# Narrower expert slots in a fused attention and mixture-of-experts layer: 32 places of 256 columns for 16 of 512

## The chip, the core and the metric

The kernel runs on one core of a Trainium2 chip. The core has a matrix engine (TensorE, PE in the profile, with its weight loads as PEld), a vector engine (DVE), a scalar engine (ACT), GpSimd (POOL) and SyncE (SP), which here only starts transfers. The metric is the device time of one execution in microseconds. Every number format on the matrix engine here is 32 bit; each product is made of three passes over a high and a low part of the operands.

## The reference

The input is 8 sequences of 512 tokens with 512 features. Attention and its two layer norms come first; nothing of that part is touched. The second half, for 4096 tokens, 8 experts and two picks a token, is:

```python
logits = x @ router_weight.T
probs = softmax(logits);  top_v, top_i = top_k(probs, 2);  top_v = top_v / top_v.sum(-1)
for e in range(8):                       # I_MOE = 352
    gu = x @ gate_up_proj[e].T
    gate, up = gu[:, :352], gu[:, 352:]
    out += (silu(gate) * up @ down_proj[e].T) * combine[:, e:e+1]
out += sigmoid(x @ shared_gate_w.T) * (silu(x @ sh_gate_w.T) * (x @ sh_up_w.T) @ sh_down_w)   # 1408 wide
```

## The kernel before

Four stages follow one another, each in a block of its own with a barrier between: attention, routing (`build_routing`), experts (`build_experts`), the shared expert (`build_shared`).

**Slots and places.** Each of the 8192 picks gets a slot, so that the slots of one expert are contiguous within a tile. How many picks an expert has is known only at run time; the widths of the tiles are fixed in the program. Routing cuts the picks of an expert into whole tiles of TS = 512 and a rest, gives the whole tiles the first places (16 of them, `FULL`), and the rests, largest first, the last seven, whose widths 448, 384, ... 64 are what the j-th largest rest can at most be. `NT` is the number of places (23), `BLOCKS` the number of 128-slot blocks of each, `SC` their sum (80). Routing computes in one chain of small VectorE steps the expert of each place (elements NT x 8) and the slot of each pick, and then the inverse, token of slot, with 64 matmuls of SC columns (L1112). GpSimd first fills constants, among them one by one `place_base` and `tile_place` (L1078, L1080), NT memsets each.

**The expert stage.** `PLACE_OF` is the order in which places are worked on: 8 full ones in a loop of pairs (`LOOPED`), then written out, rests and full ones in turn. A tile n of w slots goes as follows.

- GpSimd gathers the rows of xn of its tokens, one indirect transfer for each block of 128 (L1466), into `xg`, two tiles ahead.
- TensorE transposes them (L1274), 4 transposes a block, in groups T0 to T3 for the four chunks of 128 features. ScalarE copies each chunk out as the high part (L1280, `high_x`), VectorE subtracts to get the low part (L1285, `low_x`). There is one `xT`, so this can only be written after the last gate and up product of the tile before has read it.
- Gate and up for three chunks c of the 352 hidden rows: 2 x 12 matmuls of w columns for each c (L1251). ScalarE takes silu (L1294), VectorE multiplies and splits (L1301, L1308, L1310).
- Down: 3 matmuls of 512 columns for each block and c (L1263), into `out_ps`; ScalarE copies each block to `y_out` (L1547), and SyncE stores it to `ys`.
- Meanwhile the weights of tile n + 1 are split into high and low parts, in seven pieces on ScalarE (L1357) and VectorE (L1361); the weights of tile n + 2 are loaded by SyncE, three transfers of together 2.1 MB, issued behind the store of tile n - 1 (L1343 to L1346).

The order of TensorE in a turn is written out by hand: gate and up 0, gate and up 1, down 0, gate and up 2, T0 and T1 of the next tile, down 1, T2 and T3, down 2. T2 and T3 wait for the split of hidden chunk 2 (their banks). The first gate and up product of tile n + 1 waits for all four `low_x` of tile n + 1. VectorE's order at the end of a turn is: multiply and split hidden chunk 2, two weight pieces, four `low_x`; ScalarE's: silu of chunk 2, two weight pieces, four `high_x`, the copies of the output.

**The seam to the shared stage.** In the last turn SyncE issues the first loads of the shared stage: x of sequences 0 and 1 (4 transfers of 1 MB, `load_x`, L1385) and the first two weight chunks (6 transfers of 256 KB, `load_weights`, L1391 to L1393), and behind them the store of the last tile.

Of the kernel before, what the change touches and what calls it, by code (L numbers as in the profile page):

```python
# [26 lines left out]
P = 128  # L27
S = 512
# [34 lines left out]
def blocks_before(n):  # L63

    return BLOCKS_BEFORE[n] if isinstance(n, int) else QT * n


def width(n):
    return WIDTH[n] if isinstance(n, int) else TS


def blocks(n):
    return BLOCKS[n] if isinstance(n, int) else QT

# [930 lines left out]
def build_routing(nc, logits, gate, weight, slot, token_of_slot, tile_expert, weights):  # L1005
# [6 lines left out]
    with ctx:  # L1012
# [105 lines left out]
        def _(dve):  # L1118
# [44 lines left out]
            steps.then_wait(nc.vector.tensor_copy(whole_i[:, 2, :], n_of))  # L1163
            nc.vector.tensor_scalar(whole_i[:, 0, :], whole_i[:, 2, :], TS.bit_length() - 1, None, ALU.logical_shift_right)
            steps.then_wait(nc.vector.tensor_scalar(whole_i[:, 1, :], whole_i[:, 2, :], TS - 1, None, ALU.bitwise_and))
            nc.vector.tensor_copy(ends[0][:], whole_i[:, 0, :])
# [30 lines left out]
            steps.then_wait(nc.vector.tensor_reduce(shift_rest[:], at_place[:], AX_X, ALU.add))  # L1197
            steps.then_wait(nc.vector.tensor_scalar(whole[:, 0, :], whole[:, 0, :], float(TS), None, ALU.mult))
            steps.then_wait(nc.vector.tensor_tensor(shift_rest[:], shift_rest[:], whole[:, 0, :], ALU.subtract))
            steps.then_wait(nc.vector.tensor_scalar(shift_whole[:], first[:], float(TS), None, ALU.mult))  # L1200
            steps.then_wait(nc.vector.tensor_tensor(shift_rest[:], shift_rest[:], shift_whole[:], ALU.subtract))
# [194 lines left out]
def build_experts(nc, xn, weights, ys, token_of_slot, stored, stage, idf):  # L1396

    ctx = ExitStack()
    with ctx:
# [6 lines left out]
        rows, NC, WN, TURN = weights.ROWS, weights.NC, weights.WN, weights.TURN  # L1406
        xg = [sb(f"xg{r}", [P, QT, D]) for r in range(2)]
        index = [sb(f"index{r}", [P, QT], U32) for r in range(2)]
        xT = [sb(f"xT{j}", [P, C, TS], F32R) for j in range(2)]
        silu = [sb(f"silu{r}", [P, TS]) for r in range(2)]  # L1410
        act_s = [[sb(f"act{r}{j}", [P, TS], F32R) for j in range(2)] for r in range(2)]
        y_out = stage.yk[1]
# [19 lines left out]
        @block.sync  # L1432
        def _(sp):
            def store(n):
                sp.wait_ge(s["out_taken"], blocks_before(n) + blocks(n))
                if isinstance(n, int):
                    at = PLACE_COLUMN[PLACE_OF[n]]
                    sp.dma_start(ys[:, at:at + BLOCKS[n], :], y_out[:, 0:BLOCKS[n], :]).then_inc(stored, 16)
                else:
                    sp.dma_start(ys[:, bass.ds(QT * n, QT), :], y_out[:]).then_inc(stored, 16)  # L1440
# [41 lines left out]
        def _(pe):  # L1482
            g = GatedProducts(nc, pe, rows, xT, act_s, gate_up_ps, out_ps, s)
            pe.wait_ge(gathered[0], 16 * QT)
            for c in range(C):
                g.transpose_x(xg[0], c, idf)

            def turn(n, r, pair):
# [358 lines left out]
```

## Time and profile before

| | |
|---|---|
| median of 3 runs | 2177.38 us (2176.03 to 2180.34) |
| profiled execution | 2180.47 us, of it the span of the trace 2178.7 us |
| attention | 0 to 762 us |
| end of attention and routing | 762 to 877 us |
| expert stage, first gate product to last down product | 877.10 to 1424.23 us, 547.1 us |
| shared stage | 1429.5 us to the end |
| PE, DVE, ACT, POOL busy over the span | 91%, 48%, 32%, 22% |

The span runs from the first to the last instruction, and the time of the execution is 1.8 us longer. The page gives shares over the whole span. What one tile of the expert stage costs is read in the timeline of TensorE, one row for a run of like matmuls, and from the rows of the other engines between them.

### The profile page before, as it was taken

The numbers are of one execution on the slowest core, as the hardware profiler recorded it, in microseconds if no ns is written. First come the engines' busy times: TensorE is split into PE (matmuls) and PEld (weight loads), VectorE is DVE, ScalarE is ACT, GpSimd is POOL, SyncE is SP. The second block draws the span as 40 slices with busy tenths as digits, with TensorE's granted clock in tenths as the row PEclk, the third lists the DMA queues.
The fourth block names the chain that finished last, engine by engine and source line by source line (L and its number), as shares of the span: only waits on it lengthen the run. The fifth ranks groups of instructions, "written<-read, shape, count | busy, mean of one in ns | idle before, by whom it ended". The sixth has DMA issues, their size and how long they took to land. (4 is left out here: it accounts for less than half of the span.)

```text
span 2178.7 us, 30973 instructions
## 1 busy us (share of the span) xinstructions
PE 1989.7 (91%) x10858; PEld 1520.2 (70%) x10858; DVE 1037.5 (48%) x2158; ACT 700.6 (32%) x1350; POOL 468.4 (22%) x1045
## 2 busy tenths in 40 slices
PE   4989999999998723999999999999999999999995
PEld 3665656656666413777788888878888788888884
DVE  4556766666665328444445555443432424334243
ACT  3445545454454210344444444332111111111111
POOL 1223424233333221111111111001112021120212
PEclk9799999999998855999999999999999999999998
DMA  5134353343532213344445545332023020230202
GB/s 174 54 106 129 112 181 116 123 143 113 184 108 95 97 77 130 127 156 156 156 143 197 202 145 203 146 122 83 20 97 116 21 97 20 97 116 20 97 20 97
DMA packets 107019, 250.36 MB, mean 115 GB/s; under 512 B 10753, under 2 KB 25345, under 8 KB 99617
## 3 DMA queue, kind: packets, MB, share of 16 engines
q1 hardware_dynamic: 95392, 211.14, 28.4%
q0 software_dynamic: 11520, 37.76, 5.5%
q8 instruction: 72, 1.18, 0.2%
q14 instruction: 35, 0.28, 0.0%
HBM read 165.76 MB, written 79.69 MB: 113 GB/s over the span
## 5 line engine op out<-in xcount | busy, mean ns | idle before, releaser
L1251 PE MATMUL ex_bank<-ex_xT,ex_gu 128*128 128x512 f32 (+14 forms) x1656 | 346.8, 368 | 5.4 <-DVE ex_xT L1285 5.4
L1251 PEld LDWEIGHTS ex_bank<-ex_xT,ex_gu 128*128 128x128 f32 (+1 forms) x1656 | 277.9, 183 | 70.4 <-DVE ex_xT L1285 5.9
L1301 DVE TENSOR_TENSOR sh_silu<-sh_silu,sh_bank 128x512 f32<-128x512 f32 x88 | 60.5, 688 | 459.7 <-ACT sh_silu L1294 453.4
L1251 PE MATMUL sh_bank<-sh_xT,sh_gate 128*128 128x512 f32 x1056 | 256.3, 392 | 7.2 <-DVE sh_dn L1707 5.2
L1263 PE MATMUL sh_bank<-sh_dn,sh_act 128*128 128x512 f32 x1056 | 254.3, 390 | 0.0
L1251 PE MATMUL sh_bank<-sh_xT,sh_up 128*128 128x512 f32 x1056 | 253.6, 389 | 0.0
L671 DVE TENSOR_REDUCE at_nmax<-at_bank 128x1 fp32r<-128x384 f32 (+3 forms) x512 | 222.3, 476 | 61.2 <-PE at_bank L432 60.8
L1294 ACT ACTIVATE sh_silu<-sh_bank 128x512 f32<-128x512 f32 x88 | 52.6, 598 | 593.7 <-PE sh_bank L1251 540.8
L1251 PEld LDWEIGHTS sh_bank<-sh_xT,sh_gate 128*128 128x128 f32 x1056 | 199.6, 189 | 50.0 <-issue 8.4
L1263 PEld LDWEIGHTS sh_bank<-sh_dn,sh_act 128*128 128x128 f32 x1056 | 197.6, 188 | 43.7 <-DVE sh_act L1310 2.9
L1251 PEld LDWEIGHTS sh_bank<-sh_xT,sh_up 128*128 128x128 f32 x1056 | 198.2, 188 | 41.2
L863 ACT ACTIVATE at_PT<-at_bank 128x512 f32<-128x512 f32 (+1 forms) x384 | 184.2, 506 | 127.4 <-PE at_bank L445 102.8
L1263 PE MATMUL ex_bank<-ex_dn,ex_act 128*128 128x512 f32 (+1 forms) x720 | 183.5, 402 | 0.0
L1301 DVE TENSOR_TENSOR ex_silu<-ex_silu,ex_bank 128x512 f32<-128x512 f32 (+15 forms) x69 | 41.7, 605 | 271.1 <-ACT ex_silu L1294 271.1
L1263 PEld LDWEIGHTS ex_bank<-ex_dn,ex_act 128*128 128x128 f32 (+1 forms) x720 | 132.5, 190 | 27.5 <-DVE ex_act L1310 0.2
L445 PE MATMUL at_bank<-at_Qs,at_KsT 97*128 97x512 f32 (+3 forms) x512 | 124.9, 358 | 28.4 <-ACT at_PT L863 19.1
L967 POOL TENSOR_SCALAR_AFFINE_SELECT at_PT<-at_PT 128x384 f32<-128x384 f32 x128 | 67.0, 523 | 290.7 <-ACT at_PT L863 290.6
L1294 ACT ACTIVATE ex_silu<-ex_bank 128x512 f32<-128x512 f32 (+15 forms) x69 | 36.7, 533 | 287.3 <-PE ex_bank L1251 287.3
L428 PE MATMUL at_bank<-at_KsS,at_Qs 96*128 96x384 f32 (+3 forms) x512 | 122.8, 349 | 6.6 <-DVE at_nmax L671 5.7
L445 PEld LDWEIGHTS at_bank<-at_Qs,at_KsT 97*128 97x128 f32 x512 | 85.5, 199 | 58.9 <-ACT at_PT L863 22.6
L397 PE MATMUL at_bank<-at_xT,at_wq 128*128 128x512 f32 x384 | 95.4, 398 | 9.7 <-DVE at_q_h L631 9.2
L540 PE MATMUL at_bank<-at_wo,at_OT 128*128 128x512 f32 x384 | 98.0, 400 | 4.2 <-DVE at_y L692 2.5
(228 smaller groups left out, 2567.7 us busy)
## 6 DMA issues: line engine op xcount, KB each, us to landing
ex_gu_in<-gu_in SPq DMA_DIRECT2D x23, 1408.0 KB, 9.1
at_Qs<-q_dram SPq DMA_DIRECT2D x96, 256.0 KB, 4.1
ys<-sh_yk SPq DMA_DIRECT2D x17, 1024.0 KB
q_dram<-at_q_h SPq DMA_DIRECT2D x64, 256.0 KB, 3.8
xnT<-at_xT SPq DMA_DIRECT2D x16, 1024.0 KB, 5.0
sh_xT<-xnT SPq DMA_DIRECT2D x16, 1024.0 KB
ex_dn_in<-dn_in SPq DMA_DIRECT2D x23, 512.0 KB, 9.8
at_x_in<-x_in SPq DMA_DIRECT2D x8, 1024.0 KB, 5.3
```

The source lines that it names most:

```text
L397: last = nc.tensor.matmul(out, w[i][:, c, cols], xT[j][:, c, :], start=(n == 0), stop=(n == 3 * C - 1))
L428: nc.tensor.matmul(S_ps[u][:, col:col + (i + 1) * P], Qs[0:QK, s, i * P:(i + 1) * P], KsS[:, 0:(i + 1) * P], start=((i, col) == S_UNITS[u] ...
L445: last = nc.tensor.matmul(T_ps[tb][:, col:col + w], KsT[:, j * P:(j + 1) * P], Qs[:, h, j * P:S], start=((j, col) == tiles[0]), stop=((j, ...
L540: last = nc.tensor.matmul(F_ps[:], OT[j][:, c, i * P:(i + 1) * P], wo_s[k][:, c, :], start=(c == 0 and n == 0), stop=(c == C - 1 and n == 2))
L671: last = nc.vector.tensor_reduce(nmax[:, s % 2, i:i + 1], S_ps[u][:, col:col + (i + 1) * P], AX_X, ALU.max, negate=True)
L863: nc.scalar.activation(PT[g % 2][:, h % HG, TFROM[tb]:TFROM[tb] + TW[tb]], T_ps[tb][:, 0:TW[tb]], ACT.Exp).then_inc(pt_ready, 1)
L967: nc.gpsimd.affine_select(out=diagonals, in_=diagonals, compare_op=ALU.is_ge, fill=0.0, base=0, pattern=[[0, QT - 1], [1, P]], channel_mul ...
L1251: last = self.nc.tensor.matmul(self.gate_up_ps[c % 2][which][0:m, 0:w], cols(i, k), self.xT[j][:, k, 0:w], start=(step == 0), stop=(step = ...
L1263: last = self.nc.tensor.matmul(self.out_ps[i][:], self.act[c % 2][j][0:m, i * P:(i + 1) * P], weights(k), start=(c == 0 and step == 0), st ...
L1294: nc.scalar.activation(silu[c % 2][0:m, 0:w], gate_up_ps[c % 2][0][0:m, 0:w], ACT.Silu).then_inc(s["silu_ready"], 1)
L1301: nc.vector.tensor_tensor(silu[c % 2][0:m, 0:w], silu[c % 2][0:m, 0:w], gate_up_ps[c % 2][1][0:m, 0:w], ALU.mult).then_inc(s["product"], 1)
```

## The change

- The whole tiles become 256 slots (`TE`), 32 of them; the rests 224, 192, ... 32. `NT` is 39 for 23, `SC` 74 for 80, and the sum of the widths 9088 for 9984. The names `TS` and `QT` stay at 512 and 4 for the shared stage; the expert stage takes `TE` and `QE = 2`.
- 24 places run in the loop (12 turns of the pair, for 4), then come 15 written out: 224, 256, 32, 256, 64, 256, 96, 256, 128, 256, 160, 256, 192, 256, 256.
- In the last turn but one SyncE issues x of sequence 0 and the two weight chunks; in the last turn x of sequence 1.

The order of work within a turn is the same. Core of the diff:

```diff
-FULL = 2 * NB * S // TS
-PLACE_WIDTH = [TS] * FULL + [TS * (E - 1 - j) // E for j in range(E - 1)]
+TE = 256
+QE = TE // P
+FULL = 2 * NB * S // TE
+PLACE_WIDTH = [TE] * FULL + [TE * (E - 1 - j) // E for j in range(E - 1)]
...
-LOOPED = 8
-PLACE_OF = [*range(LOOPED), FULL, 8, FULL + 6, 9, FULL + 5, 10, FULL + 4, 11, FULL + 3, 12, FULL + 2, 13, FULL + 1, 14, 15]
+LOOPED = 24
+PLACE_OF = [*range(LOOPED)]
+for j in range(E - 1):
+    PLACE_OF += [FULL + (E - 1 - j) % (E - 1), LOOPED + j]
+PLACE_OF += [*range(LOOPED + E - 1, FULL)]
...
-            nc.vector.tensor_scalar(whole_i[:, 0, :], whole_i[:, 2, :], TS.bit_length() - 1, None, ALU.logical_shift_right)
+            nc.vector.tensor_scalar(whole_i[:, 0, :], whole_i[:, 2, :], TE.bit_length() - 1, None, ALU.logical_shift_right)
...
-        xg = [sb(f"xg{r}", [P, QT, D]) for r in range(2)]
+        xg = [sb(f"xg{r}", [P, QE, D]) for r in range(2)]
...
-                elif n == NT - 1:
-                    for b in range(2):
-                        stage.load_x(sp, b, b)
+                elif n == NT - 2:
+                    stage.load_x(sp, 0, 0)
                     for c in range(2):
                         stage.load_weights(sp, c)
+                else:
+                    stage.load_x(sp, 1, 1)
                 store(n)
```

**TensorE, one turn in the loop.** L1251 (L1257 in the change) is gate and up, L1263 (L1269) down, L1274 (L1280) the transposes of the next tile. Before:

```order
L1251 MATMUL ex_bank<-ex_xT,ex_gu 128x512 x48
L1260 ISA
L1263 MATMUL ex_bank<-ex_dn,ex_act 128x512 x12
L1251 MATMUL ex_bank<-ex_xT,ex_gu 96x512 x24
L1509 ISA
L1511 REGISTER_ALU
L1274 MATMUL ex_bank<-idf,ex_xg 128x128 x8
L1263 MATMUL ex_bank<-ex_dn,ex_act 128x512 x12
```

In the change:

```order
L1257 MATMUL ex_bank<-ex_xT,ex_gu 128x256 x48
L1265 REGISTER_ALU
L1266 ISA
L1269 MATMUL ex_bank<-ex_dn,ex_act 128x512 x6
L1257 MATMUL ex_bank<-ex_xT,ex_gu 96x256 x24
L1516 ISA
L1518 REGISTER_ALU
L1280 MATMUL ex_bank<-idf,ex_xg 128x128 x4
L1269 MATMUL ex_bank<-ex_dn,ex_act 128x512 x6
```

The order stays; the gate and up products are as many and half as wide, and down products and transposes are half as many.

**VectorE, the end of a turn** (the written-out tiles near the end of the stage). L1301, L1308 and L1310 (L1307, L1314, L1316) are hidden chunk 2, L1361 (L1367) the last two weight pieces, L1285 (L1291) the four `low_x`. Before:

```order
L1301 TENSOR_TENSOR ex_silu<-ex_silu,ex_bank 96x512
L1308 CAST ex_act<-ex_silu 96x512
L1310 TENSOR_TENSOR ex_act<-ex_silu,ex_act 96x512
L1361 TENSOR_TENSOR ex_dn<-ex_dn_in,ex_dn 128x512
L1361 TENSOR_TENSOR ex_dn<-ex_dn_in,ex_dn 96x512
L1285 TENSOR_TENSOR ex_xT<-ex_bank,ex_xT 128x512 x4
```

In the change:

```order
L1307 TENSOR_TENSOR ex_silu<-ex_silu,ex_bank 96x256
L1314 CAST ex_act<-ex_silu 96x256
L1316 TENSOR_TENSOR ex_act<-ex_silu,ex_act 96x256
L1367 TENSOR_TENSOR ex_dn<-ex_dn_in,ex_dn 128x512
L1367 TENSOR_TENSOR ex_dn<-ex_dn_in,ex_dn 96x512
L1291 TENSOR_TENSOR ex_xT<-ex_bank,ex_xT 128x256 x4
```

The activations halve, the two weight pieces stay as large as they are.

**SyncE at the seam.** `ys` is the store of a tile, `sh_xT` the x of the shared stage, `sh_f` and `sh_yk` its first two weight chunks. Before:

```order
L1438 DMA ys<-sh_yk 128x3x512
L1438 DMA ys<-sh_yk 128x4x512
L1385 DMA sh_xT<-xnT 128x2048 x4
L1391 DMA sh_f<-shg_in 128x4x128
L1392 DMA sh_f<-shu_in 128x4x128
L1393 DMA sh_f<-shd_in 128x2x256
L1391 DMA sh_yk<-shg_in 128x4x128
L1392 DMA sh_yk<-shu_in 128x4x128
L1393 DMA sh_yk<-shd_in 128x2x256
L1438 DMA ys<-sh_yk 128x4x512
```

In the change:

```order
L1444 DMA ys<-sh_yk 128x2x512
L1391 DMA sh_xT<-xnT 128x2048 x2
L1397 DMA sh_f<-shg_in 128x4x128
L1398 DMA sh_f<-shu_in 128x4x128
L1399 DMA sh_f<-shd_in 128x2x256
L1397 DMA sh_yk<-shg_in 128x4x128
L1398 DMA sh_yk<-shu_in 128x4x128
L1399 DMA sh_yk<-shd_in 128x2x256
L1444 DMA ys<-sh_yk 128x2x512
L1391 DMA sh_xT<-xnT 128x2048 x2
L1444 DMA ys<-sh_yk 128x2x512
```

The loads stand on both sides of the store of the last tile but one, instead of between it and the last.

## Rows read from the trace of the kernel before

**Rows 1.** Windows: us, busy PE PEld DVE ACT POOL, granted clock, DMA share, GB/s.

```profile
877.10:1424.23 547.13, 543.23 (x2680) 445.06 (x2680) 266.10 (x449) 221.72 (x394) 72.68 (x92) 0.99 0.46 161
...
1143.19:1160.28 17.09, 16.20 (x99) 14.99 (x97) 9.53 (x20) 8.40 (x17) 0.74 (x2) 0.70 0.58 205
...
1264.90:1280.30 15.40, 14.63 (x107) 13.42 (x105) 10.73 (x20) 9.39 (x18) 2.74 (x4) 1.00 0.77 261
```

**Rows 2.** Timeline, TensorE, looped 512 tiles: start, us, engine, line, operation.

```profile
1039.61 11.25 PE L1251 MATMUL ex_bank<-ex_xT,ex_gu 128*128 128x512 f32 x48
...
1066.34 11.25 PE L1251 MATMUL ex_bank<-ex_xT,ex_gu 128*128 128x512 f32 x48
```

**Rows 3.** Timeline, TensorE, the 256 rest and the next start; idle before in brackets.

```profile
1264.90 5.88 PE L1251 MATMUL ex_bank<-ex_xT,ex_gu 128*128 128x256 f32 x48
...
1274.84 1.03 PE L1274 MATMUL ex_bank<-idf,ex_xg 128*128 128x128 f32 x8
1275.63 1.64 PE L1263 MATMUL ex_bank<-ex_dn,ex_act 128*128 128x512 f32 x6
1277.10 1.03 PE L1274 MATMUL ex_bank<-idf,ex_xg 128*128 128x128 f32 x8
...
1280.30 11.32 PE L1251 MATMUL ex_bank<-ex_xT,ex_gu 128*128 128x512 f32 x48 [0.77 <-DVE ex_xT L1285]
```

**Rows 4.** Timeline, ScalarE and VectorE, the end of the same 256 rest.

```profile
1275.04 0.38 ACT L1294 ACTIVATE ex_silu<-ex_bank 96x256 f32<-96x256 f32 x1 [2.64 <-PE ex_bank L1251]
...
1275.45 0.42 DVE L1301 TENSOR_TENSOR ex_silu<-ex_silu,ex_bank 96x256 f32<-96x256 f32 x1 [0.93 <-ACT ex_silu L1294]
...
1275.90 0.29 DVE L1308 CAST ex_act<-ex_silu 96x256 fp32r<-96x256 f32 x1
...
1277.77 2.47 DVE L1285 TENSOR_TENSOR ex_xT<-ex_bank,ex_xT 128x512 fp32r<-128x512 f32 x4
```

**Rows 5.** Timeline, VectorE, the four low_x ahead of the 256 rest.

```profile
1262.28 1.41 DVE L1285 TENSOR_TENSOR ex_xT<-ex_bank,ex_xT 128x256 fp32r<-128x256 f32 x4
```

**Rows 6.** Timeline, VectorE, hidden chunk 2 of the last looped tile.

```profile
1086.58 0.68 DVE L1301 TENSOR_TENSOR ex_silu<-ex_silu,ex_bank 96x512 f32<-96x512 f32 x1 [5.04 <-ACT ex_silu L1294]
1087.39 0.42 DVE L1308 CAST ex_act<-ex_silu 96x512 fp32r<-96x512 f32 x1
```

**Rows 7.** Timeline, TensorE, the 128 rest and the next start.

```profile
1185.80 5.47 PE L1251 MATMUL ex_bank<-ex_xT,ex_gu 128*128 128x128 f32 x48
...
1193.88 1.06 PE L1274 MATMUL ex_bank<-idf,ex_xg 128*128 128x128 f32 x8
...
1198.90 11.32 PE L1251 MATMUL ex_bank<-ex_xT,ex_gu 128*128 128x512 f32 x48 [1.70 <-DVE ex_xT L1285]
```

**Rows 8.** Timeline, TensorE, the 64 rest and the next start.

```profile
1143.19 6.23 PE L1251 MATMUL ex_bank<-ex_xT,ex_gu 128*128 128x64 f32 x48
...
1154.40 1.97 PE L1274 MATMUL ex_bank<-idf,ex_xg 128*128 128x128 f32 x8
...
1160.28 11.35 PE L1251 MATMUL ex_bank<-ex_xT,ex_gu 128*128 128x512 f32 x48 [0.89 <-DVE ex_xT L1285]
```

**Rows 9.** Timeline, all engines, start of routing and one of its place-by-expert steps.

```profile
807.11 0.82 POOL L1078 MEMSET ro_place_base<- 128x1 f32 x23
...
825.71 0.35 DVE L1186 TENSOR_TENSOR ro_over<-ro_over 128x184 f32<-128x184 f32 x1
```

**Rows 10.** Timeline, GpSimd and TensorE, from the first gathers to the first gate product.

```profile
861.79 1.11 POOL L1466 DMA_INDIRECT ex_xg<-xn,ex_index  x1 [0.30 <-issue]
...
871.94 3.67 PE L1274 MATMUL ex_bank<-idf,ex_xg 128*128 128x128 f32 x16 [13.99 <-DMA ex_xg<-xn,ex_index]
877.10 13.34 PE L1251 MATMUL ex_bank<-ex_xT,ex_gu 128*128 128x512 f32 x48 [1.49 <-DVE ex_xT L1285]
```

**Rows 11.** Gather queue: packets, MB, share; stretches 859.8 to 865 and to 871.

```profile
q0 software_dynamic: 162, 0.54, 35.7%
...
q0 software_dynamic: 322, 1.08, 31.7%
```

More of the change, by code:

```diff
@@ L63, in blocks_before @@
 def blocks_before(n):
[L65 removed]
+    return BLOCKS_BEFORE[n] if isinstance(n, int) else QE * n
 def width(n):
[L69 removed]
+    return WIDTH[n] if isinstance(n, int) else TE
 def blocks(n):
[L73 removed]
+    return BLOCKS[n] if isinstance(n, int) else QE
 PASSES = ((0, 0), (0, 1), (1, 0))
@@ L1197, in _ @@
             steps.then_wait(nc.vector.tensor_reduce(shift_rest[:], at_place[:], AX_X, ALU.add))
-            steps.then_wait(nc.vector.tensor_scalar(whole[:, 0, :], whole[:, 0, :], float(TS), None, ALU.mult))
+            steps.then_wait(nc.vector.tensor_scalar(whole[:, 0, :], whole[:, 0, :], float(TE), None, ALU.mult))
             steps.then_wait(nc.vector.tensor_tensor(shift_rest[:], shift_rest[:], whole[:, 0, :], ALU.subtract))
-            steps.then_wait(nc.vector.tensor_scalar(shift_whole[:], first[:], float(TS), None, ALU.mult))
+            steps.then_wait(nc.vector.tensor_scalar(shift_whole[:], first[:], float(TE), None, ALU.mult))
             steps.then_wait(nc.vector.tensor_tensor(shift_rest[:], shift_rest[:], shift_whole[:], ALU.subtract))
@@ L1406, in build_experts @@
         rows, NC, WN, TURN = weights.ROWS, weights.NC, weights.WN, weights.TURN
-        xg = [sb(f"xg{r}", [P, QT, D]) for r in range(2)]
[L1408 to L1411, printed above, removed]
+        xg = [sb(f"xg{r}", [P, QE, D]) for r in range(2)]
+        index = [sb(f"index{r}", [P, QE], U32) for r in range(2)]
+        xT = [sb(f"xT{j}", [P, C, TE], F32R) for j in range(2)]
+        silu = [sb(f"silu{r}", [P, TE]) for r in range(2)]
+        act_s = [[sb(f"act{r}{j}", [P, TE], F32R) for j in range(2)] for r in range(2)]
         y_out = stage.yk[1]
@@ L1457, in gather @@
             def gather(n, r, uses):
-                columns = (bass.ds(QT * n, QT) if not isinstance(n, int) else
+                columns = (bass.ds(QE * n, QE) if not isinstance(n, int) else
                            slice(PLACE_COLUMN[PLACE_OF[n]], PLACE_COLUMN[PLACE_OF[n]] + BLOCKS[n]))
@@ L1508, in turn @@
                         else:
-                            pe.wait_ge(gathered[1 - r], 16 * QT * (pair + 1 + r))
-                            ahead = QT
+                            pe.wait_ge(gathered[1 - r], 16 * QE * (pair + 1 + r))
+                            ahead = QE
                         pe.wait_ge(s["act_ready"], NC * n + NC - 1)
@@ L1526, in _ @@
             for c in range(C):
-                high_x(nc, 0, c, xT, gate_up_ps, s)
+                high_x(nc, 0, c, xT, gate_up_ps, s, TE)
             def turn(n, r, pair):
                 last = n == NT - 1 if isinstance(n, int) else False
-                ahead = WIDTH[n + 1] if isinstance(n, int) and not last else TS
+                ahead = WIDTH[n + 1] if isinstance(n, int) and not last else TE
                 q = 0
@@ L1555, in _ @@
             for c in range(C):
-                low_x(nc, 0, c, xT, gate_up_ps, s)
+                low_x(nc, 0, c, xT, gate_up_ps, s, TE)
             def turn(n, r, pair):
                 last = n == NT - 1 if isinstance(n, int) else False
-                ahead = WIDTH[n + 1] if isinstance(n, int) and not last else TS
+                ahead = WIDTH[n + 1] if isinstance(n, int) and not last else TE
                 q = 0
```

8 lines of the change are left out of this document (4 added, 4 removed).

## The prediction

> **What bounds the kernel now.** I read the busy shares by stage first, then TensorE's timeline tile by tile, then the other engines around the end of a tile. In the expert stage TensorE is busy 543.2 of 547.1 us [rows 1], and a looped tile of 512 takes 26.73 us from one first gate product to the next (1066.34 - 1039.61), without an idle moment [rows 2]. So a full tile is bound by matmul work. Behind a narrow rest that isn't so: TensorE waits 0.77 us behind the 256 rest [rows 3] and 1.70 us behind the 128 rest [rows 7], both times for VectorE's `low_x`. The reader should see in [rows 3, 4] that the 256 rest is the new full tile, but for the tile ahead of it, which was 512 wide. The sum below is built on it.
>
> **A full tile of 256, followed by another.** From its start to the first transpose (T0) it is 1274.84 - 1264.90 = 9.94 us [rows 3]: 72 gate and up products and down 0. Two ways lead on from T0, and the later one sets the next start.
> TensorE's own: T0 and T1 took 0.79 us with eight transposes, four take 0.4; down 1 is 1277.10 - 1275.63 = 1.47; T2 and T3 again 0.4, down 2 1.47 [rows 3]. Together 3.7, a tile of 13.7 us.
> VectorE's: silu of hidden chunk 2, its multiply and split, two weight pieces, then the four `low_x`, which began at 1277.77, 2.93 us behind T0 [rows 3, 4]. None of this narrows with the tile ahead. The four took 2.47 us at 512 [rows 4] and take 1.41 at 256 [rows 5]; TensorE starts 0.06 later (1280.30 against 1277.77 + 2.47). Together 4.40.
> So VectorE ends last, and a tile is 9.94 + 4.40 = 14.34 us, of which TensorE waits some 0.7. That wait stands behind no full tile before, and the change puts it behind every one.
> Two small things come on top. A start behind a wait costs TensorE 0.07 us (48 products 11.32 [rows 3] against 11.25 without a wait [rows 2]). In the loop the cast follows the multiply 0.13 us behind its end [rows 6], written out 0.03 [rows 4]; I add 0.10 to VectorE's way. A looped tile is then 14.51 us, a written-out one 14.41.
>
> **The expert stage, summed.**
> - 24 looped tiles: 24 x 14.51 = 348.2.
> - Of the eight full ones written out, seven are followed by 32, 64, 96, 128, 160, 192 and 256. The four `low_x` cost (2.47 - 1.41) / 256 = 0.0041 us for each column ahead [rows 4, 5], so 14.41 less 0.13 for every 32 columns fewer: 13.62, 13.75, 13.88, 14.01, 14.14, 14.41 from 64 up, and 13.5 before the 32, where TensorE's own way is as late. Sum 97.3. The last has no transposes: 10.01 to T0's place, down 1 and a down 2 that waits for hidden chunk 2, 3.4: 13.4.
> - Rests: the 128 rest was 13.10 us from start to start [rows 7]; with 256 ahead for 512 it is 1.06 shorter, with the start behind a wait 12.1. Its products are paced by something other than columns: 8.08 us to T0 against 9.94 for twice the columns [rows 3, 7]. So 96, 64 and 32 at full clock gain little, 12.0, 11.9, 11.8. 160, 192 and 224 I put on the line from 12.1 to 14.4: 12.7, 13.3, 13.8. Sum 87.6.
> - The first tile runs partly at the lower clock, as now: its first 48 products 13.34 for 11.25 [rows 2, 10]. +2.1.
> Together 348.2 + 97.3 + 13.4 + 87.6 + 2.1 = 548.6 us, against 547.1 now [rows 1]: the 9% fewer columns (9088 for 9984) are eaten by waits and floors. Of the 547.1 one loss by the clock is already part, which comes now.
>
> **The clock under the narrow rests.** The 64 rest had a mean granted clock of 0.70 [rows 1]: of 17.09 us some 10.2 ran at 1.2 GHz for 2.4. It took 11.21 us to T0 against 8.08 for the 128 rest, which kept the full clock, and 5.88 from T0 to the next start against 5.02 [rows 7, 8]: some 4 us. The change has rests of 32, 64 and 96. The 32 feeds the array half as many columns as the 64, so it will fall; the 64 as before; the 96 lies between a rest that fell and one that didn't, and I take it as falling, since a wait of TensorE now also stands ahead of it. 3 x 4 = 12 us, bounds 4 (one) and 16 (the 128 too). Stage 560.6, +13.5.
>
> **Routing and the start.** Each of the steps over places and experts has 312 elements for 184, and there are ten in the chain. One took 0.35 us at 184 [rows 9]; the same kind of subtraction or product took 0.42 at 256 [rows 4], 0.001 us an element, so +0.12 each, +1.3. GpSimd's two fills are 39 memsets for 23, at 0.82 / 23 = 0.035 us [rows 9]; VectorE waits for the constants: +1.1. The inverse has 74 columns for 80, on eight VectorE steps -0.05 each: -0.4. Together +2.0.
> The first tile then waits for two gathers, not four. TensorE was released at 871.94 [rows 10]. The queue had moved 0.54 MB by 865.0 and 1.08 MB by 871.0 [rows 11]; one gather is 0.26 MB, so two were in by 865.0, all four by 871.0, before the release by 0.9. The two are released by 865.9: -6.0. From there to the first gate product it was 877.10 - 871.94 = 5.16 us, through 16 transposes and four `low_x` of 512 wide, of which the last ones count; with half of each I get 3.0: -2.2. If the weights of tile 2 mix with the gathers as they did with the last two, half of the 6.0 is lost. Taken: 2.0 - 6.0 - 2.2 = -6.1.
>
> **What costs nothing.** A load of weights (2.1 MB) comes each 14.4 us for each 26.7. The DMA engines were busy 0.77 of the 15.40 us of the 256 rest [rows 1], 11.9 us, with a store and a gather of a 512 tile among it; the new tile has half of these, and 14.4 us. The load is issued some 1 us into a tile and is wanted only when silu of chunk 0 of the next tile is done, 3 us into it. Its cover is thus 16 us; if it weren't enough, ScalarE and VectorE would be late by the excess in each tile. The seam: 5.5 MB of first loads at the 261 GB/s of the 256 rest [rows 1] need 21 us; one tile of 13.4 wouldn't cover that, the last two, 27.8, do. So the first product of the shared stage comes as late behind the last down product as now: 0. Without the cover it would be up to 8 us. Stores, output copies and gathers halve and lie beside TensorE's work.
>
> **A rule beside a row.** The gate products of the 256 rest stood between 0.118 and 0.122 us apart: (9.94 - 1.47) / 72 with a down part taken off, 5.88 / 48 with the tail of the last [rows 3]. The Trainium skill ("TensorE: Matmul & The Clock Gate", "Back-to-back issue gap") gives N / 2.4 + 2.5 ns, 109 ns at N = 256, and says that weight loads come on top at small N; as an estimate by that page 72 products would be some 0.7 us a tile shorter, 22 us in all. The trace doesn't agree with the bare formula, and the row decides.
>
> **Sum.** Stage +13.5, start -6.1: +7.4 us. Against the profiled execution, 2180.5 (span 2178.7 and 1.8 around it), that is 2187.9; its time lay 3.1 above the median, so against 2177.4 it is 2184.8, +0.34%.
>
> **The rivals.**
> - The clock holds. If only the 32, or only it and the 64, fall, the stage is +5.5 or +9.5 and the sum -0.6 or +3.4: 2176.8 to 2180.8, no difference. For it: the 128 rest kept its clock with waits of 1.7 us behind it [rows 1, 7]. Against: the 64 fell at once. Chance 0.17.
> - TensorE stays the bound. If VectorE's end of a tile came with or before TensorE's own 13.7 us, 31 tiles would each be 0.7 shorter, -22: 2163, faster. It decides at 3.7 us behind T0; VectorE would have to gain 0.7 of 4.40. For it speaks little: VectorE was idle 0.93 us before that last part already [rows 4], so no backlog falls away that could give it back. The same time would come if gate products ran nearer to their columns (107 ns at 2.4 GHz): 72 x 0.01 x 31 = 22, which is what the page's formula would give. Chance 0.08 for both.
> - The weights come late. If a load with its store and gathers needs the 15.4 us in which the 256 rest lived with 11.9 us of DMA work, each of the 31 full tiles is 1 us longer: +31, 2216. It decides when a load lands over 3 us into the next tile. Chance 0.07.
> - The start gives nothing (the gathers wait as long for their data): 6 us more, 2191. Chance 0.08.
> The forecast as summed has 0.60.
>
> **The numbers.** A measurement here can tell about 0.2%, 4.4 us, from no change. The forecast's own spread: 0.05 us a tile (2), a clock loss more or less (4), half of the start (4), added as squares 6, so 2179 to 2191, with a tail on either side; of its chance 0.12 lies within 0.2%. Slower 0.60 - 0.12 + 0.07 + 0.08 = 0.63; within 0.2% 0.12 + 0.17 = 0.29; faster 0.08. The range 2174 to 2196 takes in the first and the last rival with 3 to 5 us of their own spread, and leaves out the second and third, 0.15.
>
> **What would show it.** Looped tiles of 14.5 us with a wait for `low_x` of 0.7 before each; the first gate product near 871; a granted clock near 0.7 in the rests of 32, 64 and 96 and at 1.0 in the 128; the first shared product 5.2 us behind the last down product. The forecast is wrong if the wait behind a looped tile is missing, names a DMA, or if tiles aren't within 0.2 of 14.5.

## The result and the profile after

The changed kernel took 2184.83 us (median of 9 runs, 2177.42 to 2189.08) against 2177.38 us before (median of 9, 2171.94 to 2180.34): a ratio of 1.0034, 95% interval 1.0021 to 1.0047. It is slower by a third of a per cent. The forecast was 2184.8 us. The profiled execution took 2188.99 us, its span is 2187.2 us at a mean granted clock of 0.943, for 2178.7 us and 0.948 before.

The new kernel's lines: gate and up L1257, down L1269, transposes L1280, `high_x` L1286, `low_x` L1291, silu L1300, multiply and split L1307 to L1316, weight pieces L1363 (ScalarE) and L1367 (VectorE).

**The start.** TensorE's timeline and GpSimd's, to be read against [rows 10]: start, duration, line, operands and count, and in brackets the idle time and what ended it.

```profile
863.93 0.19 POOL L1468 CAST ex_index<-token_of_slot 128x2 uint32<-128x2 int32 x1 [50.03 <-POOLq L1018]
...
870.34 1.97 PE L1280 MATMUL ex_bank<-idf,ex_xg 128*128 128x128 f32 x8 [7.21 <-DMA ex_xg<-xn,ex_index]
...
873.32 2.07 PE L1257 MATMUL ex_bank<-ex_xT,ex_gu 128*128 128x256 f32 x8 [1.01 <-DVE ex_xT L1291]
```

From the cast of the first index to the release of TensorE it is 870.34 - 863.93 = 6.41 us; before it was 871.94 - 858.74 = 13.20. From the release to the first gate product 2.98 us, for 5.16. The absolute times can't be laid side by side, since attention ended at another moment in this execution. The first operation of routing on GpSimd is a fixed point that helps:

```profile
810.02 0.14 POOL L1080 IOTA ro_first_place<- 128x8 f32 x1 [23.04 <-POOLq L182]
...
810.32 1.34 POOL L1084 MEMSET ro_place_base<- 128x1 f32 x39
...
830.24 0.48 DVE L1192 TENSOR_TENSOR ro_over<-ro_over 128x312 f32<-128x312 f32 x1
```

It stood at 806.83 before, so attention was 3.2 us later. From it to the index cast: 53.91 us for 51.91. From it to the first gate product: 63.30 us for 70.27, a gain of 7.0.

**A looped tile.** TensorE's timeline of a tile near the end of the loop, to be read against [rows 2, 3], and below it the same end of a tile on VectorE:

```profile
1181.86 5.97 PE L1257 MATMUL ex_bank<-ex_xT,ex_gu 128*128 128x256 f32 x48 [0.55 <-DVE ex_xT L1291]
1187.67 1.56 PE L1269 MATMUL ex_bank<-ex_dn,ex_act 128*128 128x512 f32 x6
1189.07 2.99 PE L1257 MATMUL ex_bank<-ex_xT,ex_gu 128*96 128x256 f32 x24
1191.89 0.60 PE L1280 MATMUL ex_bank<-idf,ex_xg 128*128 128x128 f32 x4
...
1196.45 0.73 PE L1257 MATMUL ex_bank<-ex_xT,ex_gu 128*128 128x256 f32 x4 [0.55 <-DVE ex_xT L1291]
```

```profile
1193.71 1.28 DVE L1367 TENSOR_TENSOR ex_dn<-ex_dn_in,ex_dn 128x512 fp32r<-128x512 f32 x2
1194.91 1.41 DVE L1291 TENSOR_TENSOR ex_xT<-ex_bank,ex_xT 128x256 fp32r<-128x256 f32 x4
```

A tile is 14.60 us ((1225.58 - 889.86) / 23, from the start of the second to the end of the last of the loop) and ends in a wait for `low_x`, as every tile of the loop does. The waits of TensorE in the whole stage (what waited for what: us in total, times, longest):

```profile
PE ex_bank L1257 <- DVE ex_xT L1291: 17.3, 32, 1.2
PE ex_bank L1280 <- DMA ex_xg<-xn,ex_index: 7.2, 1, 7.2
PE ex_bank L1269 <- DVE ex_act L1316: 0.3, 1, 0.3
```

No wait for a transfer is among them but the first one. The same wait of L1257 was 5.4 us in five places before.

VectorE goes from chunk 2 through the two weight pieces to `low_x` without a pause, while ScalarE waits for TensorE's transposes within its `high_x`, so of the two it is VectorE that is late:

```profile
1194.32 0.66 ACT L1286 ACTIVATE ex_xT<-ex_bank 128x256 fp32r<-128x256 f32 x2 [0.27 <-PE ex_bank L1280]
```

**The stage and its rests.** The view of busy time by stretch, with PE's, PEld's, DVE's, ACT's and POOL's busy time, PE's granted clock, DMA share and GB/s: the whole stage, the loop from the first transposes of its second tile on, and the rests of 32, 64, 96 and 128 (to be read against [rows 1]).

```profile
873.32:1436.13 562.81, 545.35 (x3762) 490.31 (x3762) 360.94 (x769) 306.61 (x620) 81.12 (x106) 0.97 0.64 219
899.89:1225.58 325.69, 313.07 (x2179) 279.62 (x2177) 216.26 (x449) 189.91 (x372) 51.04 (x68) 1.00 0.64 217
1252.79:1269.00 16.21, 16.21 (x91) 15.00 (x90) 8.38 (x20) 6.92 (x16) 1.21 (x3) 0.62 0.55 183
1283.09:1298.82 15.73, 15.44 (x91) 14.22 (x90) 8.47 (x20) 7.04 (x17) 1.15 (x2) 0.67 0.55 189
1312.58:1327.42 14.84, 14.84 (x89) 13.63 (x90) 8.59 (x20) 6.93 (x15) 1.20 (x3) 0.68 0.61 200
1341.61:1353.75 12.14, 10.86 (x89) 9.74 (x89) 8.64 (x20) 7.26 (x16) 2.91 (x4) 1.00 0.80 265
```

The stage takes 562.8 us for 547.1, +15.7. TensorE now stands still for 17.5 us of it (562.81 - 545.35), where it had been idle for 3.9. Three rests run at a granted clock of 0.62 to 0.68, so for a good part at 1.2 GHz (none of the three has a bracket with a wait ahead of it in this trace); the rest of 128 stays at 2.4 GHz and is over in 12.14 us, 4 us sooner than the rest of 32.

**The seam.** The last down products end at 1434.46 + 1.67 = 1436.13, and the shared stage starts 5.24 us behind them, for 5.23 before:

```profile
1434.46 1.67 PE L1269 MATMUL ex_bank<-ex_dn,ex_act 96*128 96x512 f32 x6 [0.32 <-DVE ex_act L1316]
1441.37 1.19 PE L1257 MATMUL sh_bank<-sh_xT,sh_gate 128*128 128x512 f32 x2 [5.23 <-DVE sh_dn L1714]
```

So the two traces differ by -7.0 (start) + 15.7 (stage) + 0 (seam) = +8.7 us from routing to the seam. Attention (+3.2) and the shared stage (2187.2 - 1441.37 = 745.8 for 2178.7 - 1429.46 = 749.2, -3.4) cancel, and the spans differ by 8.5.

### The profile page after: what moved, and what is told of

It reads as the page before. It is cut to its first block and busy times, and to the rows that moved or that the text cites. A ratio compares the mean times of both kernels' runs of the same rounds, so it can differ in the third digit from the quotient of the medians.

```text
span 2187.2 us, 34853 instructions
## 1 busy us (share of the span) xinstructions
PE 1992.7 (91%) x11932; PEld 1564.9 (72%) x11932; DVE 1132.3 (52%) x2478; ACT 784.6 (36%) x1576; POOL 473.8 (22%) x1087
## 5 line engine op out<-in xcount | busy, mean ns | idle before, releaser
L1257 PEld LDWEIGHTS ex_bank<-ex_xT,ex_gu 128*128 128x128 f32 (+1 forms) x2808 | 343.0, 186 | 38.9 <-issue 24.1
L1257 PE MATMUL ex_bank<-ex_xT,ex_gu 128*128 128x256 f32 (+12 forms) x2808 | 352.2, 284 | 17.7 <-DVE ex_xT L1291 17.3
L1307 DVE TENSOR_TENSOR sh_silu<-sh_silu,sh_bank 128x512 f32<-128x512 f32 x88 | 60.6, 688 | 456.3 <-ACT sh_silu L1300 450.0
L1300 ACT ACTIVATE sh_silu<-sh_bank 128x512 f32<-128x512 f32 x88 | 52.6, 598 | 590.3 <-PE sh_bank L1257 537.4
L1257 PE MATMUL sh_bank<-sh_xT,sh_gate 128*128 128x512 f32 x1056 | 255.1, 391 | 5.2 <-DVE sh_dn L1714 5.2
L1269 PE MATMUL sh_bank<-sh_dn,sh_act 128*128 128x512 f32 x1056 | 254.3, 390 | 0.0
L1257 PE MATMUL sh_bank<-sh_xT,sh_up 128*128 128x512 f32 x1056 | 253.6, 389 | 0.0
L1257 PEld LDWEIGHTS sh_bank<-sh_xT,sh_gate 128*128 128x128 f32 x1056 | 199.2, 189 | 47.1 <-issue 5.6
L1269 PEld LDWEIGHTS sh_bank<-sh_dn,sh_act 128*128 128x128 f32 x1056 | 197.6, 188 | 43.7 <-DVE sh_act L1316 2.9
L1257 PEld LDWEIGHTS sh_bank<-sh_xT,sh_up 128*128 128x128 f32 x1056 | 198.2, 188 | 41.1
L1269 PE MATMUL ex_bank<-ex_dn,ex_act 128*128 128x512 f32 (+1 forms) x666 | 186.3, 414 | 0.3 <-DVE ex_act L1316 0.3
L1307 DVE TENSOR_TENSOR ex_silu<-ex_silu,ex_bank 128x256 f32<-128x256 f32 (+15 forms) x117 | 46.1, 394 | 187.1 <-ACT ex_silu L1300 187.1
L1269 PEld LDWEIGHTS ex_bank<-ex_dn,ex_act 128*128 128x128 f32 (+1 forms) x666 | 120.0, 194 | 20.2 <-DVE ex_act L1316 0.7
L1367 DVE TENSOR_TENSOR ex_gu<-ex_gu_in,ex_gu 128x704 fp32r<-128x704 f32 x156 | 131.5, 884 | 0.7 <-PEq L1018 0.6
L1363 ACT ACTIVATE ex_gu<-ex_gu_in 128x704 fp32r<-128x704 f32 x156 | 114.2, 785 | 27.1 <-DMA ex_dn_in<-dn_in 27.1
L1300 ACT ACTIVATE ex_silu<-ex_bank 128x256 f32<-128x256 f32 (+15 forms) x117 | 42.6, 364 | 226.1 <-PE ex_bank L1257 226.1
```

The costliest lines, as they stand in the source:

```text
L1257: last = self.nc.tensor.matmul(self.gate_up_ps[c % 2][which][0:m, 0:w], cols(i, k), self.xT[j][:, k, 0:w], start=(step == 0), stop=(step = ...
L1269: last = self.nc.tensor.matmul(self.out_ps[i][:], self.act[c % 2][j][0:m, i * P:(i + 1) * P], weights(k), start=(c == 0 and step == 0), st ...
L1300: nc.scalar.activation(silu[c % 2][0:m, 0:w], gate_up_ps[c % 2][0][0:m, 0:w], ACT.Silu).then_inc(s["silu_ready"], 1)
L1307: nc.vector.tensor_tensor(silu[c % 2][0:m, 0:w], silu[c % 2][0:m, 0:w], gate_up_ps[c % 2][1][0:m, 0:w], ALU.mult).then_inc(s["product"], 1)
L1363: self.nc.scalar.activation(self.piece(q, r, 0), self.piece(q, r), ACT.Copy).then_inc(self.hi, 1)
L1367: self.nc.vector.tensor_tensor(self.piece(q, r, 1), self.piece(q, r), self.piece(q, r, 0).bitcast(F32), ALU.subtract).then_inc(self.lo, 1)
```

## Experiments

The theory: in a full tile VectorE's work behind the first transpose is longer than TensorE's own, and that costs some 0.8 us a tile; the clock costs some 4 us in each rest under 128; the rest is as forecast. The first four runs ask what each of these is worth in the changed kernel, the last four whether they are peculiar to narrow places, and what the gathers' gain came from. Attention's length varied from trace to trace by up to 8 us with the same code (the first operation of routing stood anywhere between 802.3 and 810.7 us), and the kernel before had a median of 2174.70 us beside the first four runs and 2177.42 beside the last four. So the stretches within a trace are read first, and the ratios to the kernel before second.

**1. narrow_late.** The changed kernel, but the last two weight pieces of each tile, on ScalarE and VectorE, come behind the output copies and behind `low_x`. TensorE starts a tile when five pieces are there and waits for all seven ahead of down 0.

```diff
-                pe.wait_ge(weights.lo, WN * n + WN)
+                pe.wait_ge(weights.lo, WN * n + WN - len(TURN[NC - 1]))
...
                     if c > 0:
+                        if c == 1:
+                            pe.wait_ge(weights.lo, WN * n + WN)
                         down(c - 1)
...
                 if not last:
                     for c in range(C):
                         low_x(nc, n + 1, c, xT, gate_up_ps, s, ahead)
+                    for _ in TURN[NC - 1]:
+                        weights.split_lo(n + 1, 1 - r, q)
+                        q += 1
```

> The changed kernel, with one edit: the last two weight pieces of a turn (of down chunks 1 and 2) are split by ScalarE behind its output copies and by VectorE behind the four low_x, no longer between hidden chunk 2 and low_x; TensorE starts a tile on five pieces and waits for all seven before down 0. Theory (VectorE's end of a turn holds back the next tile by some 0.6 us, 32 times): VectorE's way shortens by the two pieces, 1.28 us, so TensorE's own way is the later one; looped tiles 14.6 -> 13.8 to 13.9 us, the wait for low_x gone, stage some 20 us shorter, 2164 to 2167 in all. Rival (the tiles are long because TensorE starts slowly behind any wait, or because the weight loads crowd it): looped tiles stay above 14.4, 2180 or more.

Measured: 2156.91 us, ratio to the kernel before 0.9917 (0.9899 to 0.9936). TensorE's timeline, a looped tile; and its waits in the stage:

```profile
885.95 5.88 PE L1257 MATMUL ex_bank<-ex_xT,ex_gu 128*128 128x256 f32 x48
891.67 1.56 PE L1269 MATMUL ex_bank<-ex_dn,ex_act 128*128 128x512 f32 x6
...
899.74 0.99 PE L1257 MATMUL ex_bank<-ex_xT,ex_gu 128*128 128x256 f32 x7
```

```profile
PE ex_bank L1257 <- DVE ex_xT L1291: 2.0, 4, 1.0
```

The tile is 13.79 us and has no bracket with a wait: 0.81 less than 14.60. From the first gate product to the first shared product the trace has 1412.69 - 870.10 = 542.6 us, for 568.05 in the changed kernel: -25.5, of which 24 x 0.81 = 19.4 in the loop and the other 6 in the tiles written out. The order of two pieces on two engines is thus worth 25 us, and TensorE's own 13.7 us is what remains. The gain was bigger than the 20 us expected since the written-out tiles gain too. Note that the waits view gave this wait 17.3 us, less 2.0 that stayed: it showed 15 of the 25. In a looped tile the bracket was 0.55 us and the gain 0.81, of which 0.09 is the slower start behind a wait (5.81 for 5.72 us to down 0). PE's ends are modelled and reach into the wait, so the bracket is too small; starts alone are safe. The edit moves pieces on two engines at once and wasn't tried on one alone.

The rests fell nonetheless, with no wait of TensorE ahead of them (16.40, 15.67 and 14.05 us). So a wait ahead isn't what costs them the clock. They also show a pace: the first 48 products of the rest of 96, at a granted clock of 1.00, took 1294.26 - 1288.96 = 5.30 us, as long as 48 products of 128 columns (1321.91 - 1316.60 = 5.31).

**2. narrow_pad.** The changed kernel, but the rests of 32, 64 and 96 are worked on with 128 columns, the further ones empty.

```diff
-WIDTH = [PLACE_WIDTH[p] for p in PLACE_OF]
+WIDTH = [max(P, PLACE_WIDTH[p]) for p in PLACE_OF]
```

> The changed kernel, with the rests of 32, 64 and 96 columns worked at 128 columns (they have one block of 128 slots anyway; only the width of the products and copies changes). Theory (these three are slow because the granted clock falls, and their products are paced by something other than columns): the clock stays at 1.0 in all four, each takes about 12.1 us for 16.2, 15.7 and 14.8, so -10 us, 2174 to 2177. Rival (the pace or the clock goes by the number of products, not their width): each stays as long or grows with the columns, 2185 to 2190.

Measured: 2172.53 us, ratio 0.9991 (0.9979 to 1.0003). The rest of 32, now at 128 columns, in TensorE's timeline, and the three rests in the view by stretch:

```profile
1245.60 5.58 PE L1257 MATMUL ex_bank<-ex_xT,ex_gu 128*128 128x128 f32 x48 [0.15 <-DVE ex_xT L1291]
...
1257.74 0.50 PE L1257 MATMUL ex_bank<-ex_xT,ex_gu 128*128 128x256 f32 x2 [1.17 <-DVE ex_xT L1291]
```

```profile
1245.60:1257.74 12.14, 10.86 (x89) 9.74 (x89) 8.64 (x20) 7.26 (x16) 1.97 (x3) 1.00 0.72 245
1271.64:1283.78 12.14, 10.86 (x89) 9.74 (x89) 8.64 (x20) 7.26 (x16) 1.96 (x3) 1.00 0.71 244
1297.68:1309.82 12.14, 10.86 (x89) 9.73 (x89) 8.64 (x20) 7.26 (x16) 1.96 (x3) 1.00 0.71 245
```

Each of the three is as long as the real rest of 128. Four, two and one and a third times the columns take 4.1, 3.6 and 2.7 us less. From gate to shared the stretch is 557.7 us, -10.3. Here TensorE waits 1.17 us behind each rest and keeps 2.4 GHz; in narrow_late it waited at most 0.34 us behind one and lost it. The Trainium skill ("TensorE: Matmul & The Clock Gate", "HAM oscillation — how this bites in real kernels") lays such losses to idle gaps between groups of matmuls, in a kernel that waits for its transfers. These traces show a loss without any gap that the profile has (PE's ends are modelled): the rest of 32 above has PE busy for 16.21 of 16.21 us at a clock of 0.62, so the measurement decides. In this pair of runs the width and the waits around a rest change together; the next run keeps the waits out.

**3. narrow_late_pad.** Both edits.

> Both edits together. Theory: they act in different tiles and add, 2154 to 2158, faster than both kernels. Rival: what one gives the other takes (TensorE closer to its own work in the 256 tiles uncovers late weights, or narrow tiles behind them lose the clock again), 2162 or more.

Measured: 2149.27 us, ratio 0.9878 (0.9856 to 0.9900). The stretch from gate to shared is 1403.65 - 874.10 = 529.6 us, -38.5 against the changed kernel, for 25.5 + 10.3 = 35.8 apart. The 2.7 more are the rests: without the two pieces ahead of `low_x` a rest of 128 columns takes 11.21 us, not 12.14, and there are three more of these now. The rest of 32 in the view by stretch, in narrow_late and here:

```profile
1229.50:1245.90 16.40, 16.40 (x91) 15.19 (x89) 8.64 (x20) 7.13 (x16) 0.99 (x3) 0.61 0.52 181
1233.23:1244.44 11.21, 10.78 (x91) 9.63 (x89) 8.82 (x20) 7.39 (x17) 0.95 (x3) 1.00 0.74 263
```

Neither has a wait of TensorE ahead of it, and behind the rest there is none in narrow_late and 0.34 us here. The rests of 64 and 96 are the closest pair: none ahead and 0.34 us behind in narrow_late, where they fall, and none ahead and 0.35 behind here, where they hold. What differs is the number of columns that is worked on. This version beats both kernels, by 1.2% the one before.

**4. narrow_seam.** The changed kernel, but all first loads of the shared stage stand in the last turn, as before the change.

```diff
-                elif n == NT - 2:
-                    stage.load_x(sp, 0, 0)
+                elif n == NT - 1:
+                    for b in range(2):
+                        stage.load_x(sp, b, b)
                     for c in range(2):
                         stage.load_weights(sp, c)
-                else:
-                    stage.load_x(sp, 1, 1)
```

> The changed kernel, with all first loads of the shared stage in the last turn again, as in the kernel before. Theory (5.5 MB at 261 GB/s need 21 us, the last tile gives 13.5): the first product of the shared stage comes 4 to 8 us later behind the last down product than the 5.2 us it has now; 2189 to 2192. Rival (the engines move over 350 GB/s when nothing else runs, and the weights needed first are small): within 1 us of 5.2, no difference.

Measured: 2186.87 us, ratio 1.0057 (1.0040 to 1.0074). TensorE and ScalarE at the seam:

```profile
1438.11 1.19 PE L1257 MATMUL sh_bank<-sh_xT,sh_gate 128*128 128x512 f32 x2 [7.18 <-DVE sh_dn L1713]
```

```profile
1434.37 0.63 ACT L1675 ACTIVATE sh_gate<-sh_f 128x512 fp32r<-128x512 f32 x1 [2.80 <-DMA sh_f<-shd_in]
```

The shared stage starts 7.2 us behind the last down product (at 1430.94), for 5.24: 2.0 us, and ScalarE's first split now waits for a load of weights. Both expectations miss, the one high and the other low. The ratio doesn't speak against it (0.0023 or 5 us more, with intervals that overlap). The load of a tile sooner is needed, but it is worth 2 us. When SyncE issued the first of the loads, when ScalarE had the second chunk of weights, and the last split of the first chunk on VectorE:

```profile
1418.00 2.49 SPq L1391 DMA_DIRECT2D sh_xT<-xnT  x4
1436.59 0.63 ACT L1675 ACTIVATE sh_gate<-sh_yk 128x512 fp32r<-128x512 f32 x1 [0.55 <-DMA sh_yk<-shd_in]
1437.28 0.68 DVE L1713 TENSOR_TENSOR sh_dn<-sh_f,sh_dn 128x512 fp32r<-128x512 f32 x1
```

The first chunk was in 16.4 us behind the issue, all 5.5 MB 18.6 us, and TensorE started 0.15 us behind the split of the first chunk (1438.11 for 1437.96).

**5. wide_late.** The kernel before with the edit of narrow_late.

> The kernel before the change (16 places of 512), with the same edit of the two weight pieces. Theory (a 512 tile is bound by TensorE's own work and has no wait to give back; only the tiles behind narrow rests wait for low_x, 5.4 us in all): looped tiles stay at 26.73 us, some 3 to 5 us faster than before, so the edit is worth a sixth of the 25 us that it is worth with places of 256. Rival (the edit helps whatever the width, by a shorter way for weights or output): 15 us or more.

Measured: 2174.92 us, ratio 0.9989 (0.9971 to 1.0007). TensorE's waits for `low_x` in the stage, the kernel before first:

```profile
PE ex_bank L1251 <- DVE ex_xT L1285: 5.4, 5, 1.7
```

```profile
PE ex_bank L1251 <- DVE ex_xT L1285: 3.6, 5, 1.5
```

A looped tile stays at 26.73 us, and gate to shared is 548.5 us for 552.4: -3.9. But half of that isn't the edit's. The first 48 products of the stage took 13.34 us in the kernel before [rows 10], partly at the lower clock, and ran at full clock here:

```profile
872.66 11.37 PE L1251 MATMUL ex_bank<-ex_xT,ex_gu 128*128 128x512 f32 x48 [1.49 <-DVE ex_xT L1285]
```

From the first start to the second it is 26.88 us for 28.84, which is 2.0 of the 3.9. The edit changes nothing ahead of that start, and wide_gather below, without this edit, ran at full clock there too. The other 1.9 agree with the waits (5.4 to 3.6). So the same edit that gave 25.5 us in the narrow kernel gives some 2 here, since a tile of 512 had no wait to take away.

**6. wide_pad.** The kernel before with the rest of 64 at 128 columns.

> The kernel before the change, its rest of 64 columns worked at 128. Theory (one loss of the clock, some 4 us, goes): 3 to 4 us faster than before, granted clock 1.0 in that rest. Rival (the fall of the clock was by chance or by the place in the order): the clock falls at 128 columns too, no difference.

Measured: 2175.87 us, ratio 0.9978 (0.9964 to 0.9991). The padded rest goes from 17.09 to 13.11 us, -4.0. But gate to shared is only 2.6 us shorter, for in this execution the clock fell in the full tile behind the second rest of 128: its first 48 products took 12.88 us, where the tile behind the padded rest needed 11.32. The granted clock was 0.85 over 1195.72 to 1207.04, and 1.00 over 1157.13 to 1168.30, behind the padded rest.

```profile
1144.02 5.47 PE L1251 MATMUL ex_bank<-ex_xT,ex_gu 128*128 128x128 f32 x48
1149.33 0.92 PE L1263 MATMUL ex_bank<-ex_dn,ex_act 128*128 128x512 f32 x3
1150.09 2.18 PE L1251 MATMUL ex_bank<-ex_xT,ex_gu 128*96 128x128 f32 x24
1152.11 1.06 PE L1274 MATMUL ex_bank<-idf,ex_xg 128*128 128x128 f32 x8
...
1195.72 12.88 PE L1251 MATMUL ex_bank<-ex_xT,ex_gu 128*128 128x512 f32 x48 [1.69 <-DVE ex_xT L1285]
```

The first four rows also show what paces narrow products. From start to start, 48 products whose weights have 128 columns take 1149.33 - 1144.02 = 5.31 us, 0.111 each, and the 24 whose weights have 96 columns 1152.11 - 1150.09 = 2.02, 0.084 each, all of them with 128 moving columns. With 256 moving columns both kinds take the same: 5.81 / 48 = 0.121 and 2.82 / 24 = 0.118 in the looped tile above. So at 128 it is the weight load that sets the pace, at 256 the moving operand. The Trainium skill ("TensorE: Matmul & The Clock Gate", "LDWEIGHTS (loading the stationary operand)") gives a load P / 1.2 ns, 107 and 80 ns for 128 and 96 columns; these rows agree to 4 ns. Without the page the rows say it too: 0.084 to 0.111 is as 96 to 128.

**7. wide_late_pad.** The kernel before with both edits.

> The kernel before the change with both edits, to set against the narrow places with both. Theory: 6 to 9 us faster than before, and so some 17 to 20 us slower than places of 256 with both edits (ratio to before 0.996 to 0.997 against 0.988): the width pays only once VectorE's end of a turn is out of the way. Rival: both edits bring the two widths to the same gap as without them (narrow 0.3% slower).

Measured: 2172.91 us, ratio 0.9972 (0.9957 to 0.9986); gate to shared 543.6 us, -8.7, of which 2.0 again are the first tile at full clock (its first 48 products took 11.31 us). One of its ten executions took 6525 us and is no part of the ratio; what held it up isn't known. With both edits the narrow places come to 0.9878 and the wide ones to 0.9972, some 20 us apart. In the traces 14.0 us of the distance lie from gate to shared (529.6 for 543.6), 6.6 in routing and the start, and 2.5 in the shared stage, whose code is the same (attention's length takes part of it back). So the narrower place is the better one by itself, by 2.6% of the stage where its 9% fewer columns would promise more, and the changed kernel loses because two things stand against it.

**8. wide_gather.** The kernel before, but SyncE's first load of weights, 2.1 MB for tile 2, waits until the four gathers of the first tile are in.

```diff
                 if not isinstance(n, int) or n + 2 < NT:
+                    sp.wait_ge(gathered[0], 16 * QT)
                     sp.wait_ge(weights.lo, WN * n + WN)
```

> The kernel before the change, SyncE starts the load of weights of tile 2 only when the four gathers of tile 0 have landed. Theory (the third and fourth gather come late because that load runs among them; this is why two fewer gathers gave 6.8 us): TensorE is released 2 to 3 us earlier behind the index than 13.2 us, about 10.5, the whole 2 to 3 us faster. Rival (each gather takes its time, 1.25 us to issue and the rest to land, with or without the load): 12.7 to 13.2 us, no difference.

Measured: 2176.06 us, ratio 0.9991 (0.9975 to 1.0006). GpSimd's cast of the index and TensorE's release:

```profile
857.96 0.19 POOL L1462 CAST ex_index<-token_of_slot 128x4 uint32<-128x4 int32 x1 [49.09 <-POOLq L1012]
```

```profile
867.40 3.68 PE L1274 MATMUL ex_bank<-idf,ex_xg 128*128 128x128 f32 x16 [10.25 <-DMA ex_xg<-xn,ex_index]
```

9.44 us from cast to release, for 13.20 with the load among the gathers and 6.41 with two gathers. So of the 6.8 us that the change gained here, 3.8 came from getting out of the way of that load; the other 3.0 are the two further gathers. SyncE's rows, the kernel before and the changed one, show why two gathers escape it:

```profile
864.77 0.35 SPq L1343 DMA_DIRECT2D ex_gu_in<-gu_in  x1
```

```profile
869.91 0.35 SPq L1349 DMA_DIRECT2D ex_gu_in<-gu_in  x1
```

In both the load is issued 6.0 us behind the cast (858.74 and 863.93). The changed kernel's two gathers release TensorE 0.4 us later, the four of the kernel before 7.2 us later. The ratio itself doesn't stand off from 1, and the stretch from the first gate product on was only 0.5 us shorter (551.9): the first tile ran at full clock here as well, -2.0, and, again, the tile behind a rest of 128 lost the clock for a while (12.88 us for its 48 products), +1.6.

## Why the prediction was right

**A full tile.** Forecast 14.51 us in the loop, measured 14.60. The parts: start to first transpose 1191.89 - 1181.86 = 10.03 (9.94 and 0.07 forecast), from there to `low_x` 3.02 (2.93 and 0.10), `low_x` 1.41 (1.41). What was mis-sized is the last term: from the end of `low_x` to TensorE's start it is 1196.45 - 1196.32 = 0.13, not the 0.06 that I had from a written-out tile. The prediction added 0.10 for the loop on VectorE's side, but took TensorE's answer to the wait from written-out code. 24 x 0.09 = 2.1 us, as much as the stage missed (+15.7 for +13.5), but the rest of the terms only cancel: the seven rests came to 98.7 us for 99.6, the seven full tiles among them to 98.3 for 97.3. A written-out tile followed by a full one took 14.43 (14.41). That VectorE bounds the tile, and TensorE's own way is 13.7 to 13.8, is shown by narrow_late: remove VectorE's excess and the tile is 13.79.

**Rests and the clock.** The forecast was that 32, 64 and 96 fall, 128 holds, at 4 us each, with 12.1 for the 128. They took 16.21, 15.73, 14.84 and 12.14; narrow_pad shows what they cost over a rest that holds: 4.1, 3.6 and 2.7, 10.3 in all. The reason given for the 96, that a wait stands ahead of it, was wrong: the changed kernel's trace has no bracket there, and in narrow_late, where no wait is left to hide, it falls too. The right pick had a wrong reason. Two more things of this part were read too simply. The 64 didn't fall at once: its first 48 products took 6.23 us for 5.47 of the 128 [rows 7, 8], so most of them ran at full clock. And the loss doesn't end with the rest: the full tiles behind 32 and 96 began at a granted clock of 0.90 and 0.93 and took 0.3 to 0.5 us more than forecast (14.09 for 13.62, and 14.19 for 13.88). The first tile's start at the lower clock cost 889.86 - 873.32 - 14.60 = 1.9 (2.1).

**Routing and start.** Routing +2.0, as forecast: 39 fills 1.34 us, a step 0.48. Gathers -6.8 for -6.0, first tile's chain -2.2 for -2.2. The case that the weights mix with the gathers and take half of the gain didn't come. Rather the reverse: wide_gather shows that in the kernel before the load held up the last two gathers, and that 3.8 of the 6.8 us were getting out of its way.

**The seam.** 0, as forecast. The cost without the cover was put at up to 8 us and is 2.0. That number was made of 5.5 MB at 261 GB/s, 21 us, less the last tile's 13.4. In narrow_seam's trace the first chunk of weights, the one whose split the first product waits for, is in after 16.4 us (1434.37 - 1418.00), since the transfers ran faster: 410 GB/s over 1422.5 to 1430.9. The 261 was the mean of a stretch in which they had no hurry. And even with all loads in, ScalarE's first split comes 1.5 us behind the last down product (1437.62 - 1436.13), which covers a part. 1418.00 + 16.4 is 3.4 us behind the last down product at 1430.94, less 1.5: the 1.9 to 2.0 measured.

**The rivals.** The clock didn't hold (three lost). TensorE isn't the bound (waits in all tiles), though the price put on that rival, 22 us, was right: narrow_late got it, by other means, with 25.5 (19.4 in the loop). No weights came late. The start gave what it should.

**The sum.** Stage +15.7 for +13.5, start -7.0 for -6.1: +8.7 for +7.4 in the traces, and the medians differ by 7.45. That the median met the forecast so closely is luck: the stage cost 2.2 us more and the start gave 0.9 more than forecast, the shared stage, put at nothing, took 3.4 less in these traces, and from trace to trace the same code differs by up to 8 us in attention alone.

## What to carry to other kernels

When the tile of a pipelined loop is halved, what doesn't shrink with it on a helper engine (here the two weight pieces ahead of `low_x`) becomes the bound; look at what stands ahead of the operation on which the matrix engine waits, and move what isn't wanted yet behind it. Products of under 128 columns gained nothing here: their pace is that of the weight load (5.30 us for 48 of 96 columns, 5.31 for 48 of 128) and they lost the clock, so padding them to 128 was faster. Judge a wait by the distance between two starts, with and without it, not by the bracket. And before a few us between two traces are given to an edit, look for a stretch ahead of it whose clock differs.

## What was not expected of the hardware

- The clock was lost at products of 32, 64 and 96 columns with TensorE hardly standing still (0.62 in the 16.21 us of the rest of 32, PE busy throughout), and kept at 128 columns with waits of 1.17 us behind them, and with 0.35.
- The first 48 products of the stage ran partly at the lower clock in two of the five wide kernels' traces (13.34 and 13.23 us) and at full clock in the other three (11.31 to 11.37), with the same code up to there but for wide_gather's load. That is 2 us between two traces which no edit made.
- Behind a rest of 128 in the wide kernel it was lost for a while in two executions (12.88 us for 48 products, for 11.32), in wide_pad and in wide_gather, and not in others. Which condition decides stays open.
- A wait in the loop was answered 0.07 us later than the same wait in written-out code (0.13 for 0.06).
- Gathers beside a load of 2.1 MB were held up by 3.8 us of 13.2.
- The shared stage, the same code, took some 2 to 3 us less in all five kernels with narrow places (745.8 to 747.0) than in the five with wide ones (748.3 to 749.2). In the wide ones TensorE has two moments, 1.7 to 1.9 us together, in which it waits for nothing that the trace names, and none in the narrow ones. TensorE's timeline of the kernel before:

```profile
1703.10 3.01 PE L1251 MATMUL sh_bank<-sh_xT,sh_gate 128*128 128x512 f32 x12 [1.12 <-issue]
...
1884.24 3.01 PE L1251 MATMUL sh_bank<-sh_xT,sh_gate 128*128 128x512 f32 x12 [0.82 <-issue]
```

No run tells why; it went with the program around it, not with the stage.
